# One ring of six x buffers in place of two sets, and a step loop with a body of six steps instead of two

## The reference, cut to what matters

```python
x = x + attention(ctx_1024, layernorm(x), Wq, Wk, Wv, lambdas)   # 16 heads, two softmax maps each, difference
x = x + moe(layernorm(x), gate_w, w_gate, w_up, w_down, ws_gate, ws_up, ws_down)
```

## Time and profile before

| | |
|---|---|
| median of 3 runs | 2260.15 us (2256.93 to 2262.98) |
| profiled execution | 2249.22 us, span 2247.5 us |
| busy share PE / DVE / ACT / POOL | 90% / 71% / 63% / 64% |
| mean granted TensorE clock | 0.972 |
| moved by DMA | 432.05 MB, mean 192 GB/s |
| loop of steps 4 to 57 | 155.0 to 1530.3 us on PE, 27 passes of 51 us |

### The profile page before, as it was taken

How to read it: one execution, slowest core, us unless ns; L and a number is a source line. 1 busy time by engine, 2 the same in 40 slices (tenths; PEclk the granted TensorE clock), 3 DMA queues, 4 the chain that set the end, 5 groups by cost and what they waited for, 6 DMA issues and landing times.

```text
span 2247.5 us, 76469 instructions
## 1 busy us (share of the span) xinstructions
PE 2021.7 (90%) x20840; PEld 1405.2 (63%) x20840; DVE 1584.5 (71%) x4623; ACT 1426.2 (63%) x3511; POOL 1446.2 (64%) x2183
## 2 busy tenths in 40 slices
PE   4999999999999999999999999999977988889996
PEld 3666665566656566656656566666546877768775
DVE  3777777777777777778777777778765655546554
ACT  2777777777777777777776777777763444434443
POOL 4466777767677676767676767767664555545554
PEclk8899999999999999999999999999987999999999
DMA  5997777777777777777777777878846777667774
GB/s 133 222 225 192 187 195 190 178 189 184 191 190 184 186 194 185 185 183 182 191 193 178 184 188 190 194 181 216 228 173 180 223 214 214 199 178 220 220 223 127
DMA packets 616921, 432.05 MB, mean 192 GB/s; under 512 B 447811, under 2 KB 562634, under 8 KB 616400
## 3 DMA queue, kind: packets, MB, share of 16 engines
q1 hardware_dynamic: 556528, 319.91, 58.3%
q0 software_dynamic: 32256, 84.47, 11.8%
q10 hardware_dynamic: 28000, 26.03, 3.8%
HBM read 234.59 MB, written 197.72 MB: 192 GB/s over the span
## 4 chain that ended last, share of the span: by engine, by line
PE 67%; DVE 15%; issue 10%; ACT 3%; DMA 2%; SPq 1%; POOL 1%; DVEq 1%; another core or an unknown queue 1%; ACTq 0%; POOLq 0%
PE mx_ps L494 11%; PE o_ps L527 7%; DVE mx L982 6%; PE ms_ps L778 5%; PE o_ps L538 5%; PE ms_ps L555 5%; PE mx_ps L557 4%; PE mx_ps L555 4%; PE ms_ps L576 4%; PE st_ps L756 3%; PE mx_ps L556 3%; PE ms_ps L583 3%; PE st_ps L487 3%; PE ms_ps L556 3%; PE ms_ps L557 2%
## 5 line engine op out<-in xcount | busy, mean ns | idle before, releaser
L982 DVE TENSOR_REDUCE mx<-mx_ps 128x4 f32<-128x512 f32 x1024 | 686.3, 685 | 300.4 <-PE mx_ps L494 294.2
L826 ACT ACTIVATE prob<-st_ps 128x512 f32<-128x512 f32 x1024 | 604.5, 598 | 357.8 <-PE st_ps L487 353.5
L494 PE MATMUL mx_ps<-stacks 48*128 48x128 bf16 x4096 | 396.7, 221 | 67.6 <-DVE mx L982 33.8
L487 PE MATMUL st_ps<-stacks 50*128 50x128 bf16 x4096 | 394.9, 220 | 0.0
L494 PEld LDWEIGHTS mx_ps<-stacks 48*128 48x128 bf16 x4096 | 230.9, 95 | 228.6 <-issue 105.9
L527 PE MATMUL o_ps<-prob,v_sb 128*32 128x256 f32 x4096 | 331.6, 396 | 0.8 <-ACT prob L826 0.4
L1344 POOL DMA_INDIRECT rows_dram<-rowt,posi x256 | 253.7, 991 | 67.6 <-issue 64.3
L555 PE MATMUL ms_ps<-e_lo 128*128 128x256 f32 x768 | 264.7, 345 | 18.1 <-issue 11.1
L923 ACT ACTIVATE rows_T<-st_ps 128x256 fp32r<-128x256 f32 x288 | 111.7, 388 | 192.2 <-PE st_ps L756 137.3
L487 PEld LDWEIGHTS st_ps<-stacks 50*128 50x128 bf16 x4096 | 229.8, 95 | 2.5 <-issue 1.5
L1413 POOL DMA_INDIRECT sums_dram<-stacks x144 | 141.7, 984 | 130.4 <-DVE stacks L1220 70.2
(11 more groups left out here) (155 smaller groups left out, 4694.4 us busy)
## 6 DMA issues: line engine op xcount, KB each, us to landing
stack_dram<-w_dn_sb SPq DMA_DIRECT2D x768, 128.0 KB
stacks<-stack_dram SPq DMA_DIRECT2D x512, 192.0 KB
stacks<-rows_dram SPq DMA_DIRECT2D x288, 130.0 KB
w_dn_sb<-in_x SPq DMA_DIRECT2D x64, 256.0 KB
w_dn_sb<-in_ctxT SPq DMA_DIRECT2D x64, 256.0 KB
x_res<-in_x SPq DMA_DIRECT2D x64, 256.0 KB
stacks<-sums_dram SPq DMA_DIRECT2D x78, 128.0 KB
stacks<-base_dram SPq DMA_DIRECT2D x76, 128.0 KB
```

The costliest lines, as they stand in the source:

```text
L487: return pe.matmul(st_ps[k % 2][:, i * P:(i + 1) * P], k_st[p][64 * h:64 * h + KROWS, u, j, :], q_st[p][64 * h:64 * h + KROWS, u, j, :], s ...
L494: return pe.matmul(mx_ps[k % 2][:, i * P:(i + 1) * P], q_st[p][64 * h:64 * h + ROWS, u, j, :], k_st[p][64 * h:64 * h + ROWS, u, j, :], sta ...
L826: nc.scalar.activation(prob[k % 4][:, :], st_ps[k % 2][:, :], ACT.Exp, scale=float(HALF) ** -0.5).then_inc(a_exp, 1)
L982: v.tensor_reduce(mx[:, u, c * CHUNK:(c + 1) * CHUNK], mx_ps[k % 2][:, :].rearrange("p (c n) -> p c n", c=CHUNK), AX.X, ALU.max).then_inc( ...
```

## The change

x gets one ring of six buffers `x_in[0..5]`, buffer s mod 6 for pair s. It is loaded once, at the place in SP's step where the residual's load stood and under the same wait on `g_x2`, for the pair `it+5`; the norm reads it one step later and the residual six steps later (it is free again when the residual of `it-1` is done, which is the same slot of the ring). The two sets `x_res` and the wait on `a_n1` go. As the buffer's number must be known where the code is written, the loop's body becomes six steps and runs nine times.

```diff
+    def sixth(self):
+        return self.off % 6
...
-        x_in, xn = (ahead[:, i * 512:(i + 1) * 512].rearrange("p (u d) -> p u d", u=2) for i in range(2))
+        xn = ahead[:, 0:512].rearrange("p (u d) -> p u d", u=2)
...
-        x_res = [sb(f"x_res{i}", [P, 2, D]) for i in range(2)]
+        x_in = [sb(f"x_in{i}", [P, 2, D]) for i in range(6)]
...
-        d_w, d_x, d_c = sem("d_w"), sem("d_x"), sem("d_c")
+        d_w, d_c = sem("d_w"), sem("d_c")
...
-        d_res = [sem(f"d_res{i}") for i in range(2)]
+        d_x = [sem(f"d_x{i}") for i in range(2)]
...
         first, lo, hi, end = -4, 4, NS - 6, NS + 3
+        assert (hi - lo) % 6 == 0
...
         def steps(eng, body):
-            pipeline(eng, body, first, lo, hi, end, 2)
+            pipeline(eng, body, first, lo, hi, end, 6)
...
-                if b.is_in(0, NS):
+                x5 = it.plus(5)
+                if x5.is_in(1, NS):
                     wait(sp, g_x2, 4, it, 0)
-                    sp.dma_start(x_res[1 - p][:, :, :],
-                                 x_g[bass.ds(b.idx(), 1)].rearrange("g p u d -> (g p) u d")).then_inc(d_res[1 - p], 16)
-                if xs.plus(1).is_in(1, NS):
-                    wait(sp, a_n1, 2, xs, 2)
-                    sp.dma_start(x_in[:, :, :],
-                                 x_g[bass.ds(xs.plus(1).idx(), 1)].rearrange("g p u d -> (g p) u d")).then_inc(d_x, 16)
+                    sp.dma_start(x_in[x5.sixth()][:, :, :],
+                                 x_g[bass.ds(x5.idx(), 1)].rearrange("g p u d -> (g p) u d")).then_inc(d_x[x5.par()], 16)
...
                     if k == 7 and do_xs:
-                        wait(act, d_x, 16, xs, 16)
+                        wait_par(act, d_x, 16, xs)
                         wait(act, p_xT, 1, xs)
-                        norm(xs, x_in, mv1, nb1, xn, g_nb1, a_n1)
+                        norm(xs, x_in[xs.sixth()], mv1, nb1, xn, g_nb1, a_n1)
...
                 if h == 0:
-                    wait_par(gp, d_res, 16, s)
+                    wait_par(gp, d_x, 16, s)
...
-                                x_res[p][:, u, m * P:(m + 1) * P].rearrange("p (h d) -> p h d", d=DH),
+                                x_in[s.sixth()][:, u, m * P:(m + 1) * P].rearrange("p (h d) -> p h d", d=DH),
```

More of the change, by code:

```diff
@@ L338, in _ @@
         def _(sp):
-            sp.dma_start(x_in[:, :, :], x_g[0]).then_inc(d_x, 16)
+            sp.dma_start(x_in[0][:, :, :], x_g[0]).then_inc(d_x[0], 16)
             sp.dma_start(c_in[:, :, :], ctxT[0]).then_inc(d_c, 16)
@@ L1123, in step @@
                     if k == 2 and do_xs:
-                        wait(dve, d_x, 16, xs, 16)
-                        stats(xs, x_in, bs1, mv1, v_b1, v_s1, a_n1)
+                        wait_par(dve, d_x, 16, xs)
+                        stats(xs, x_in[xs.sixth()], bs1, mv1, v_b1, v_s1, a_n1)
                     if k == 4 and do_d:
```

## The result

The changed kernel takes 2302.34 us (median of 4 runs, 2289.08 to 2308.52) against 2258.93 us before (4 runs): a ratio of 1.0182, 95% interval 1.0135 to 1.0229. It is slower, as forecast, and 2302 lies inside the range; but the loss is 43 us where 21 were forecast. The profiled execution is the fastest of its four (2289.08 us against 2249.22 of the one before, +39.9), and its mean granted clock is 0.957, where it was 0.972.

What follows compares the result with a forecast made beforehand. The prediction took PE's matmul stream to bound the loop, with transfers hidden. Stall 16 us plus clock 6 us minus 1 us for the x loads gave +21 us, so 2281 us against 2260.15, range 2260 to 2307.

Steps and rivals of the forecast that it cites:

- What bounded the kernel: In the loop, PE's matmul stream sets the time, DVE close behind at a few places; transfers are hidden.
- The x loads: Dropping one load per step gains nothing in the loop; warm-up statistics start 0.14 us earlier, 1 us put for all.
- PE's body is not kept: PE's six-step loop code, 15 packets or 246 KB, is fetched anew each pass, some 120 more packets in all.
- Rival A: The loop body is kept or its fetch covered, so only -1 us shows: 2259 us, no change; chance 0.17.
- rival B: Fewer bytes moved in the loop make it faster, -18 us, ending at 2242 us; chance 0.05.
- Short branches cost nothing: Eighteen fewer branches back in the loop give PE nothing; the longer body's saving is zero.
- a sign that the x loads matter: If loop steps without a branch changed their length from 25.5 us, the prediction would be wrong.
- The stall, 2.0 us per return: At each of 8 branches back, PE waits for an instruction fetch of 2.67 us, partly covered: 16 us in all.
- The clock: Half-clock stretches behind about half of the loop's returns, four at 1.5 us: 6 us, between 0 and 12.
- The range: Whole kernel at 2260 to 2307 us, holding the forecast and the lower half of Rival C.
- The other engines cost nothing: Stalls of DVE, ACT, POOL and SP at their branches back cost nothing; 4 us if DVE's cover fell short.
- Rival C: A larger stall at returns: two fetches in a row, half clock after each, or stalls not overlapping; 2309 us, chance 0.14.

Runs made afterwards that it cites:

- experiment 10: Kernel before, all 54 steps in one pass on PE alone, two-step body on the other engines: ratio 0.9998.
- experiment 12: Kernel before, all 54 steps in one pass on DVE alone, two-step body on the other engines: ratio 0.9789.
- experiment 1: Kernel before with a six-step body on all engines, both loads of x kept: 2292.62 us, ratio 1.0168.
- experiment 3: Kernel before with a six-step body on DVE, ACT, POOL and SP, two steps on PE: 2257.69 us, ratio 1.0039.
- 4: Changed kernel with PE's body at two steps, the ring and the others' six steps kept: 2262.38 us, ratio 1.0069.
- 7: Changed kernel with all 54 steps in one pass on every engine: 2197.59 us, ratio 0.9729.
- 8: Kernel before, two loads of x, with all 54 steps in one pass on every engine: 2198.30 us, ratio 0.9743.
- 2: Kernel before with a six-step body on PE alone, two steps on the other engines: 2289.16 us, ratio 1.0163.
- experiment 6: Changed kernel with an eighteen-step body, two returns: 2273.25 us, ratio 1.0061.
- 9: Kernel before with a four-step body on PE alone, twelve returns, two steps on the other engines: 2309.13 us, ratio 1.0203.

## Why the prediction came out as it did

**What bounded the kernel: right in part.** The transfers are hidden, as the prediction had it. But PE's stream of matmuls does not set the pace alone, with DVE "close behind at a few places": PE written out gains nothing (experiment 10), and DVE written out takes 0.8 us from every step (experiment 12). The sum of the prediction did not rest on this.

**The x loads: right.** No engine waits for x in the loop, and taking the second load out gives nothing (experiments 1 against the changed kernel, 3 against 4, 7 against 8). In the warm-up the x load left the chain and DVE began its statistics at 21.60 instead of 21.79 us: 0.19 us, forecast 0.14.

```profile
20.99 0.04 DVE e_lo L970
21.02 0.57 issue
21.60 0.74 DVE bs L1011 x2
```

**PE's body is not kept: right**, with 129 packets for a forecast of 120. Rival A is refuted, and with it rival B, which needed it and a wait for x that never showed.

**Short branches cost nothing: about right.** Plain steps are 0.15 us shorter in the changed kernel, 8 us in all, where zero was forecast; these runs don't tell the fewer branches from the rest of the longer body. Counted together with the low-clock stretches, steps without a return got longer, from 25.47 to 25.67 us, which the prediction had named as a sign that the x loads matter. They do not: experiment 1, with both loads, has 18 such stretches.

**The stall, 2.0 us per return: too large, but near.** The branch itself takes 3.58 us (2.67 was taken for the fetch), PE's idle time is 2.75 in the row above, and DVE is 1.8 us late. An ordinary low-clock stretch of 3.4 us makes a step 1.66 us longer. The eight returns have 3 x 3.4 + 5 x 6.8 = 44.2 us of low clock, so 5.5 us each, worth 2.7 by that rate; of the 4.0 us of a return 1.3 are left for the stall. That is an estimate, and it gives 10 us where 16 were forecast. The returns themselves bear the rate out: of the 38 in the changed kernel and experiments 1, 2, 6 and 9, the nine with 3.4 us of low clock make steps of 28.4 us, the 27 with 6.8 us steps of 29.9.

**The clock: the term that was mis-sized.** "I expect one behind about half of the returns", at 1.5 us each, 6 us in all, 12 at most. For a stretch of 3.4 us the price was right (1.4 before, 1.7 in the changed kernel). But every return has one, five of the eight are twice as long as any in the kernel before, and together they cost some 8 x 2.7 = 22 us. I had read the ordinary stretches of before and taken a return's for the same, only half as frequent; no row of before showed one behind an idle time of this kind. The other 15 us stand in steps without a return: 14 low-clock stretches instead of 6, a term that the prediction put at nothing. The sum of these terms, 10 + 22 + 15 - 8, is 39 us.

**The range: held in part by luck.** Its upper part stands for a stall of 3.65 us per return or more, with 12 us for the clock. The stall came out below its forecast, and what filled the range was the clock, with 22 us outside the 0 to 12 given to it, and the 15 us that were not in the sum at all.

**The other engines cost nothing: nearly.** With PE at two steps they cost 0.4% (experiment 3) to 0.7% (4), 9 to 16 us; beside PE's stall, no more than the intervals hide. The cover that I gave DVE, 2.42 us from one row, was the longest of 26: that idle time varies from 0.4 to 2.4 us between the passes of the kernel before. The five low-clock stretches behind these returns (experiments 3 and 4) are part of what they cost.

**Rival C** (2309) was nearest in size, and by one of its branches: a stretch at half the clock behind each return. Its other branch, two fetches in a row (37.5 us), did not happen: the stall proper is smaller than forecast.

**Open:** why the ordinary stretches went from 6 to 14. They begin 8 to 10 us behind a step's start, as before. Longer idle times at PE's returns don't explain them: experiments 3 and 4, where PE's code is kept, have 11 and 15 beside those behind returns, and PE in one pass, at the pace of before (25.27 us a plain step) and with no return, has 12; the rest in one pass has 5, and the two kernels with every engine in one pass none. It may be how the engines' streams stand against each other at that place; no run here isolates it.

## What to carry to other kernels

Before a loop's body is made longer, read from the trace how many instruction packets one pass brings and whether they stop after the first pass: a body that is kept pays nothing at its branch, one that is not pays at each return, so give each engine a body length of its own and keep PE's at what it keeps (here 5 packets of 16 KB; 10 were fetched anew). A stall of the array is to be priced with the stretch of low clock behind it, which here, by the estimate above, cost twice the stall. And if a loop outgrows the store anyway, one written-out pass has no return at all and turns register arithmetic for waits into constants; DVE alone in one pass gave 2% here, most likely by that.

## What was not expected of the hardware

After each of the 8 returns the granted clock was 0.50 for 3.4 or 6.8 us, and so it was behind all 30 returns of PE in experiments 1, 2, 6 and 9, twice for 10.2 us (one return of 6, one of 9), though PE was busy for 6.43 of 6.80 us in such a stretch. A return whose code is gone costs PE's sequencer 3.6 to 4.3 us (medians of the rows of four kernels) and up to 6.2 us (experiment 6), whether 11 or 16 packets follow it. And four engines' returns without PE's, fetches of their own included, cost the kernel 0.4 to 0.7% where PE's alone cost 1.6%.
